# Attention of a four-stage chain: value products issued for one unit at a time in place of two, with other preferences in the plan of instruction order

## The chip, the cores and the metric

The kernel runs on one core of a Trainium2 chip. The metric is device time of one execution in microseconds (us); the kernel before took 3964.82 us (median of three runs, 3960.57 to 3975.85). The profiled execution took 3958.41 us, and the span of its trace, from the first instruction to the last, is 3956.8 us.

## The reference, cut to what matters

Four layers run one after the other on 4096 tokens of 256 channels, each with a residual and a layer norm: a recurrent scan, a mixture of experts, causal attention, a second mixture of experts. The change touches attention alone:

```python
q_lat = (x @ Wq_down).reshape(b, t, H, L)      # H = 16 heads; k_lat, v_lat likewise
...
q = jnp.concatenate([q_c, _apply_rope(q_e, cos, sin)], axis=-1)   # 16 channels a head
k = jnp.concatenate([k_c, _apply_rope(k_e, cos, sin)], axis=-1)
scores = jnp.einsum('bhqd,bhkd->bhqk', q, k) * scale
scores = jnp.where(causal[None, None], scores, -jnp.inf)
att = jax.nn.softmax(scores, axis=-1)
y = jnp.einsum('bhqk,bhkd->bhqd', att, v)
```

Here b is 1 and t is 4096.

## The kernel before

Attention works on two heads at a time: eight pairs of heads, and in each pair the 4096 queries in eight chunks of 512. A *segment* is two chunks of one pair (in the middle of the stage an early one with a late one, so that each segment has the same work); there are 32. A *unit* is one chunk of 512 queries against 128 keys, for both heads; there are 1152, and a middle segment has 36. The four units of a chunk that lie on the causal diagonal use fewer columns and add a mask with two small matmuls for each head.

Each score is computed twice on TensorE. First *S* (L1598, masks at L1604): 128 queries against 512 keys, for both heads, into two PSUM banks, of which VectorE takes the row maximum (L1724). S has a ring of two such pairs of banks (RING_S), so S number i waits for the maximum of number i-2. At the end of a segment its maxima are negated, turned by a transpose (L1652), copied by ScalarE (L1683) and sent through memory into two extra rows of the queries. Then *ST* (L1622, masks at L1627): the transposed scores of one head of a unit, less the maximum, into one bank; ScalarE takes the exponential into probs_T (L1677). ST has a ring of three banks (RING_ST), shared with the transposes of the maxima, so an ST waits for the exponential three items earlier. Last *AV* (`values`, L1642): the value products, probs_T as the moving operand against 17 columns of values (16 channels and a one, which gives the sum of the row). The two heads and the two halves of the 512 queries lie in four column groups of the array, so four matmuls run side by side; each is two instructions in the trace, so a full unit has eight. In the lists of instruction order each is one, so a full unit has four there. AV waits for the exponentials of its units; an exponential waits until AV has read the buffer it writes (a ring of six units, RING_P). ScalarE copies a finished chunk out (L1689).

S and ST use 64-row parts of the array, one head in each, so two heads run side by side. AV uses all rows and 32-column parts.

In which order TensorE, ScalarE and VectorE issue all this is laid down beforehand by `attention_plan()`. It plays the stage through with estimated durations. At each step it lists what TensorE could issue next, each with its earliest start and a due time: for ST the time at which ScalarE runs out of work, for S the time at which VectorE does, for AV a fixed time from now (REACT) less a sum for each unit by which AV lags. Of those that could start within SOON of the earliest it takes the one that is due first. On the chip the order is fixed, and semaphores set the times. S may run up to two segments ahead of ST.

Of the kernel before, what the change touches and what calls it, by code (L numbers as in the profile page):

```python
# [1265 lines left out]
NSEG = NPH * len(MIDDLE)  # L1266
SEGMENTS = RISING + (NPH - 2) * MIDDLE + RISING[::-1]
RING_P = 6
WIDE_S = 2
RING_S = 2  # L1270
S_BANKS = WIDE_S * RING_S
RING_ST = 7 - S_BANKS
# [31 lines left out]
def attention_plan():  # L1304

    units, rows = attention_units()
    SEEN, SOON = 80, 200
    LATENCY, LANDED, CLOSE, REACT = 270, 6000, 900, 2500
    last_row = {n: r for r, (n, x, i, m) in enumerate(rows)}
    n_s = len(rows) * 2 // WIDE_S
    n_t = len(units) * 2
    pe, half, act, dve = 0, [0, 0], 0, 0
    st = av = s = turn = 0
    item, consumed, exped, maxed = 0, {}, {}, {}  # L1320
    av_end, o_copied, folded, landed = {}, 0, {}, {}
    order_pe, order_dve, order_act = [], [], []
    to_act, to_dve = [], []

    def stream(start, j, columns, diag):
        begin = max(start, half[j])
        half[j] = begin + 30 + 0.42 * columns + (110 if diag else 0)
        return half[j] + LATENCY

    while True:  # L1330

        while to_act or to_dve:
            queues = [(max(q[0][0], t), name) for q, t, name in ((to_act, act, "act"), (to_dve, dve, "dve")) if q]
            start, name = min(queues)
            if start >= pe:
                break
            ready, kind, x, cost = (to_act if name == "act" else to_dve).pop(0)
            end = start + cost
            if name == "act":
                act = end  # L1340
                order_act.append((kind, x))
                if kind == "EXP":
                    consumed[x[1]] = end
                    exped[x[0]] = end
                elif kind == "MCOPY":
                    consumed[x[1]] = end
                    landed[x[0]] = end + LANDED
                else:
                    o_copied = end
            else:  # L1350
                dve = end
                order_dve.append((kind, x))
                maxed[x] = end
                r, heads = heads_of_S(x)
                n = rows[r][0]
                if r == last_row[n] and heads[-1] == 1:
                    dve += CLOSE
                    order_dve.append(("MFIN", n))
                    folded[n] = dve
        can = []  # L1360
        if st < n_t and 2 * av > st // 2 - RING_P and (item < RING_ST or item - RING_ST in consumed):
            n = units[st // 2][0]
            if n in landed:
                ready = max(landed[n], consumed[item - RING_ST] + SEEN if item >= RING_ST else 0)
                can.append((max(pe, ready), act + sum(w[3] for w in to_act), "ST", st))
        if 4 * av + 3 < st and (4 * av + 3) in exped:
            n, qc, kt = units[2 * av]
            if kt or not any(w[1] == "OCOPY" for w in to_act):
                ready = max(exped[4 * av + 3], o_copied if kt == 0 else 0) + SEEN
                can.append((max(pe, ready, max(half)), pe + REACT - 100 * (st // 2 - 2 * av - 2), "AV", av))  # L1370
        if s < n_s and (s < RING_S or s - RING_S in maxed) and (st == n_t or rows[heads_of_S(s)[0]][0] <= units[st // 2][0] + 2):
            ready = maxed[s - RING_S] + SEEN if s >= RING_S else 0
            can.append((max(pe, ready), dve + sum(w[3] for w in to_dve), "S", s))
        if turn in folded and (item < RING_ST or (item - RING_ST) in consumed):
            ready = max(folded[turn], consumed[item - RING_ST] if item >= RING_ST else 0) + SEEN
            can.append((max(pe, ready), pe - 2000, "MTURN", turn))
        if not can:
            if not to_act and not to_dve:
                if landed and st < n_t and units[st // 2][0] not in landed:
                    raise ValueError("stuck")  # L1380
                return order_pe, order_act, order_dve, max(pe, act, dve)
            pe = max(pe, min(max(q[0][0], t) for q, t in ((to_act, act), (to_dve, dve)) if q)) + 1
            continue
        soonest = min(c[0] for c in can)
        pending = [max(q[0][0], t) for q, t in ((to_act, act), (to_dve, dve)) if q]
        if pending and min(pending) < soonest:
            pe = max(pe, min(pending) + 1)
            continue
        start, _, kind, x = min((c for c in can if c[0] <= soonest + SOON), key=lambda c: c[1])
        if kind == "ST":  # L1390
            n, qc, kt = units[x // 2]
            columns = CH - max(0, kt - QT * qc) * P
            ready = stream(start, head_of_T(x), columns, kt >= QT * qc)
            pe = max(start, half[head_of_T(x)] - 240) + 60
            to_act.append((ready, "EXP", (x, item), 30 + columns / 0.954))
            item += 1
            st += 1
        elif kind == "AV":
            pe = start + 60
            for n, qc, kt in units[2 * x:2 * x + 2]:  # L1400
                pe += 2 * 0.91 * min(HALF, CH - max(0, kt - QT * qc) * P)
            half[:] = [pe, pe]
            av_end[x] = pe + 100
            av += 1
            if kt == QT * qc + QT - 1:
                to_act.append((pe + 300, "OCOPY", (n, SEGMENTS[n].index(qc)), 350))
        elif kind == "S":
            r, heads = heads_of_S(x)
            n, _, i, m = rows[r]
            columns = min(CH, (i + 1) * P - m * CH)  # L1410
            for j in heads:
                ready = stream(start, j, columns, m == i // QT)
                start = max(start, half[j] - 240) + 60
            pe = start
            to_dve.append((ready, "MAX", x, (60 + len(heads) * columns) / 0.96))
            s += 1
        else:
            pe = max(start, max(half)) + 120
            half[:] = [pe, pe]
            to_act.append((pe + LATENCY, "MCOPY", (x, item), 250))  # L1420
            item += 1
            turn += 1
        order_pe.append((kind, x))


def attention(nc, k, a):
# [5 lines left out]
    units, rows = attention_units()  # L1432
# [3 lines left out]
    slots, item = {}, 0  # L1436
# [10 lines left out]
    last_row = {n: r for r, (n, x, i, m) in enumerate(rows)}  # L1447
    s_before = {n: (last_row[n] + 1) * 2 // WIDE_S for n in range(NSEG)}
    chunk_of = {(n, x): 2 * n + x for n in range(NSEG) for x in range(2)}
    last_group = {(n, SEGMENTS[n].index(qc)): u // 2 for u, (n, qc, kt) in enumerate(units)}  # L1450
    with ExitStack() as ctx:
        sb, sem = k.sbuf(ctx), k.stage_sem
        q = sb("q_rows", [P, 2, T], F32R)
# [15 lines left out]
        st_done, taken, av_done, o_copied = (sem("at_" + n) for n in ("st_done", "taken", "av_done", "o_copied"))  # L1469
# [109 lines left out]
        def _(pe):  # L1579
# [48 lines left out]
                last.then_inc(st_done, 1)  # L1628

            def values(g):  # L1630
                pe.wait_ge(taken, slots["ST", 4 * g + 3] + 1)
                for u in (2 * g, 2 * g + 1):
                    n, qc, kt = units[u]
                    c = chunk_of[n, SEGMENTS[n].index(qc)]
                    if kt == 0 and c:
                        pe.wait_ge(o_copied, c)
                    for j in range(2):
                        for half in range(2):
                            lo = max(0, max(0, kt - QT * qc) * P - HALF * half)
                            if lo < HALF:  # L1640
                                at = 32 * (2 * j + half)
                                last = pe.matmul(ps[at:at + HD + 1, 7, lo:HALF], k.v[:, kt, 2 * (n // 4) + j, :],  # L1642
                                                 pt[:, u % RING_P, j, HALF * half + lo:HALF * (half + 1)],
                                                 start=(kt == 0), stop=(kt == QT * qc + 1 + 2 * half))
                last.then_inc(av_done, 1)
# [19 lines left out]
        def _(act):  # L1665
            for c in range(4):
                load_first(act, kk, 1, (HIGH, HIGH, LOW), c)
            for kind, x in plan_act:
                if kind == "EXP":
                    t, at_item = x  # L1670
                    u, j = t // 2, head_of_T(t)
                    n, qc, kt = units[u]
                    o = max(0, kt - QT * qc) * P
                    act.wait_ge(st_done, at_item + 1)
                    if u >= RING_P:
                        act.wait_ge(av_done, (u - RING_P) // 2 + 1)
                    act.activation(pt[:, u % RING_P, j, o:CH], ps[:, S_BANKS + at_item % RING_ST, o:CH], ACT.Exp, scale=SCALE).then_inc(taken, 1)  # L1677
                elif kind == "MCOPY":
                    n, at_item = x
# [542 lines left out]
```

## Time and profile before

| | before |
|---|---|
| median of three runs | 3964.82 us |
| profiled execution, span of its trace | 3958.41 us, 3956.8 us |
| attention, from the first S to the last AV | 1630.3 to 3208.6 us |
| busy over the span: TensorE, VectorE, ScalarE | 83%, 75%, 50% |
| S matmuls, ST matmuls, AV matmuls (records) | 2304, 2304, 8704 |
| maxima on VectorE, exponentials on ScalarE | 1152, 2304 |

A matmul's record reaches from its start to a modelled end, and matmuls overlap in the array; so how long TensorE is held by one is read from the distance of one start to the next.

### The profile page before, as it was taken

Reading aid. Unit: us, or ns where it says so; the run is one execution under the profiler, and the core shown is the slowest. Engines: PE = TensorE matmul, PEld = TensorE weight load, DVE = VectorE, ACT = ScalarE, POOL = GpSimd, SP = SyncE. Lnnn points to the kernel's source line nnn. Section 1 sums busy time; section 2 is a strip of 40 time slices with the busy share of each in tenths; the row PEclk is TensorE's granted clock in tenths of the full one; section 3 lists DMA queues with packets and bytes.
Section 4 is the critical chain, followed back from the end, with each engine's and each line's share of the span. In section 5 each row is a group of like instructions: output and inputs, shape, how many; then the busy total and the mean of one; then the engine's idle time right before and its main releaser. Section 6 shows DMA issues by size and latency. Waiting matters only on the chain. (4 is left out here: it accounts for less than half of the span.)

```text
span 3956.8 us, 70342 instructions
## 1 busy us (share of the span) xinstructions
PE 3296.1 (83%) x25130; PEld 2356.1 (60%) x25130; DVE 2956.1 (75%) x5189; ACT 1989.2 (50%) x4068; POOL 1121.4 (28%) x1381
## 2 busy tenths in 40 slices
PE   4477776780799956799999999999999955999997
PEld 1477776740688855544555555555555424888886
DVE  7999999941344446688888888888889406888888
ACT  2544444410444412256777777777777832333333
POOL 2888888705222242000111111112021030000000
PEclk7788888875899967788999999999999977999999
DMA  3000000012222135520303031221200000000001
GB/s 135 1 1 0 0 0 0 0 46 105 94 85 85 53 100 158 119 38 7 45 13 45 13 45 24 36 35 26 42 18 11 9 24 9 13 12 12 12 12 43
DMA packets 85212, 150.95 MB, mean 38 GB/s; under 512 B 16625, under 2 KB 53382, under 8 KB 83251
## 3 DMA queue, kind: packets, MB, share of 16 engines
q1 hardware_dynamic: 64626, 104.12, 10.9%
q0 software_dynamic: 19584, 42.14, 3.5%
q10 hardware_dynamic: 768, 1.57, 0.3%
q8 instruction: 146, 2.39, 0.3%
q14 instruction: 88, 0.71, 0.1%
HBM read 90.60 MB, written 57.41 MB: 37 GB/s over the span
## 5 line engine op out<-in xcount | busy, mean ns | idle before, releaser
L1724 DVE TENSOR_REDUCE row_max<-psum 128x2 f32<-128x1024 f32 (+2 forms) x1152 | 1250.4, 1131 | 219.1 <-PE psum L1598 164.2
L1677 ACT ACTIVATE probs_T<-psum 128x512 f32<-128x512 f32 (+3 forms) x2304 | 1120.8, 566 | 366.0 <-PE psum L1622 283.6
L1622 PE MATMUL psum<-q_rows,k_rows 50*128 50x512 f32 (+3 forms) x2304 | 771.6, 440 | 15.1 <-ACT probs_T L1677 11.5
L379 PE MATMUL psum<-h_hist,stream 128*128 128x192 f32 x2816 | 502.8, 344 | 246.4 <-ACT h_hist L360 246.4
L1598 PE MATMUL psum<-k_rows,q_rows 48*128 48x512 f32 (+3 forms) x2304 | 641.1, 451 | 39.3 <-DVE row_max L1724 23.8
L334 POOL TENSOR_TENSOR x_times_b<-x_slab,B_sb 128x384 f32<-128x384 f32 (+1 forms) x828 | 625.4, 818 | 149.3 <-DVE psum L285 91.1
L379 PEld LDWEIGHTS psum<-h_hist,stream 128*128 128x128 f32 x2816 | 496.4, 203 | 252.7 <-ACT h_hist L360 154.6
L1642 PE MATMUL psum<-probs_T,v_all 128*17 128x256 f32 (+1 forms) x8704 | 600.3, 378 | 1.0 <-issue 1.0
L1622 PEld LDWEIGHTS psum<-q_rows,k_rows 50*128 50x128 f32 x2304 | 364.7, 187 | 328.5 <-ACT probs_T L1677 278.3
L360 ACT ACTIVATE h_hist<-psum 128x384 f32<-128x384 f32 (+1 forms) x828 | 339.4, 453 | 378.4 <-DVE psum L285 378.4
L1972 PE MATMUL psum<-x_T,w_part 128*128 128x512 f32 x1632 | 404.3, 397 | 24.8 <-POOL w_part L2032 24.8
L1598 PEld LDWEIGHTS psum<-k_rows,q_rows 48*128 48x128 f32 x2304 | 286.9, 191 | 151.7 <-DVE row_max L1724 96.3
L285 DVE TENSOR_TENSOR psum<-psum,x_times_b 128x384 f32<-128x384 f32 (+1 forms) x828 | 372.9, 508 | 0.0
L280 DVE TENSOR_TENSOR psum<-h_hist,psum 128x384 f32<-128x384 f32 (+1 forms) x828 | 371.2, 506 | 0.5 <-ACT h_hist L360 0.2
L1642 PEld LDWEIGHTS psum<-probs_T,v_all 128*17 128x17 f32 x8704 | 210.5, 97 | 259.4 <-ACT probs_T L1677 80.9
L1972 PEld LDWEIGHTS psum<-x_T,w_part 128*128 128x128 f32 x1632 | 301.0, 190 | 85.5 <-POOL w_part L2032 24.9
L1567 POOL DMA_DIRECT2D o_raw<-o_acc x64 | 37.0, 578 | 1092.1 <-ACT o_acc L1689 1057.6
L2071 DVE SCALAR_TENSOR_TENSOR stream<-psum,comb,stream 128x256 f32<-128x256 f32 x544 | 236.4, 476 | 0.6 <-PE psum L1984 0.6
L1984 PEld LDWEIGHTS psum<-w_part,hidden_T 128*128 128x128 f32 x1632 | 214.4, 192 | 28.6 <-DVE hidden_T L2057 15.6
L1984 PE MATMUL psum<-w_part,hidden_T 128*128 128x256 f32 x1632 | 219.4, 285 | 14.2 <-DVE hidden_T L2057 14.2
L832 PE MATMUL psum<-xeT_part,w_part 128*128 128x512 f32 x768 | 183.2, 398 | 25.4 <-ACT hT_part L873 12.8
L2032 POOL TENSOR_TENSOR w_part<-attn_T,w_part 128x768 fp32r<-128x768 f32 x17 | 31.5, 1853 | 599.1 <-ACT w_part L1996 493.7
(212 smaller groups left out, 3260.2 us busy)
## 6 DMA issues: line engine op xcount, KB each, us to landing
w_raw<-in_w SPq DMA_DIRECT2D x16, 1024.0 KB, 8.4
qk_rows<-qk_split SPq DMA_DIRECT2D x64, 256.0 KB, 3.0
q_rows<-qk_rows SPq DMA_DIRECT2D x42, 256.0 KB, 12.0
k_rows<-qk_rows SPq DMA_DIRECT2D x42, 256.0 KB, 16.8
inbox<-zeros SPq DMA_DIRECT2D x8, 1024.0 KB, 10.5
xe_sb<-inbox SPq DMA_DIRECT2D x8, 1024.0 KB, 6.0
outbox<-ye_sb POOLq DMA_DIRECT2D x8, 1024.0 KB, 10.4
o_raw<-o_acc POOLq DMA_DIRECT2D x64, 128.0 KB, 2.1
```

The source lines that it names most:

```text
L280: dve.tensor_tensor(part(ha, i), part(prev, i), over_chunks(A, i), ALU.mult).then_inc(ha_ready, 1)
L285: dve.tensor_tensor(u(i), part(ha, i), part(xb[:, t % RING_X], i), ALU.add).then_inc(u_ready, 1)
L334: pool.tensor_tensor(out, x, b, ALU.mult).then_inc(xb_ready, 1)
L360: act.activation(part(hist[:, slot, t], i), u(i), ACT.Tanh).then_inc(h_ready, 1)
L379: last = pe.matmul(ps[:, 1 + j, 0:BL * DH * CHUNKS], diag[:, s, :], hist[:, j, :, :, :].rearrange("p t h (s c) -> p (t h) s c", s=NS)[:, : ...
L1598: last = pe.matmul(ps[:, bank_of_S(s, j), 0:width], q[at, b, i * P:(i + 1) * P], kk[at, b, mm * CH:mm * CH + width], start=True, stop=not ...
L1622: last = pe.matmul(ps[:, bank, o:CH], kk[at, b, kt * P:(kt + 1) * P], q[at, b, qc * CH + o:(qc + 1) * CH], start=True, stop=not diag)
L1642: last = pe.matmul(ps[at:at + HD + 1, 7, lo:HALF], k.v[:, kt, 2 * (n // 4) + j, :], pt[:, u % RING_P, j, HALF * half + lo:HALF * (half + 1 ...
L1677: act.activation(pt[:, u % RING_P, j, o:CH], ps[:, S_BANKS + at_item % RING_ST, o:CH], ACT.Exp, scale=SCALE).then_inc(taken, 1)
L1724: dve.tensor_reduce(mx[:, n % 4, heads[0]:heads[-1] + 1, QT * c + i % QT, mm], ps[:, banks, 0:width], AX.X, ALU.max).then_inc(maxed, 1)
L1972: last = pe.matmul(ps[:, 2 * half + c % 2, :], w_part[:, b, wp, at:at + INTER], xT[:, xp, h, c * CH:(c + 1) * CH], start=(n == 0 and h == ...
L1984: last = pe.matmul(ps[:, 4 + 2 * (c % 2) + s // 2, (s % 2) * D:(s % 2 + 1) * D], hT[:, c % 2, hp, s * P:(s + 1) * P], w_part[:, b, wp, WCO ...
```

## The change

AV is issued for one unit in place of two (GROUP = 1), and the waits on either side follow: AV waits for two exponentials in place of four, and an exponential waits for the AV of one unit. In the plan the window in which items compete, SOON, goes from 200 to 100, the due time of AV, REACT, from 2500 to 1000, and each unit of lag brings AV forward by 300 in place of 100. The number of matmuls, maxima and exponentials is the same; lines from 1266 on move by one or two.

```diff
+GROUP = 1
...
-    SEEN, SOON = 80, 200
-    LATENCY, LANDED, CLOSE, REACT = 270, 6000, 900, 2500
+    SEEN, SOON = 80, 100
+    LATENCY, LANDED, CLOSE, REACT = 270, 6000, 900, 1000
...
-        if st < n_t and 2 * av > st // 2 - RING_P and (item < RING_ST or item - RING_ST in consumed):
+        if st < n_t and GROUP * av > st // 2 - RING_P and (item < RING_ST or item - RING_ST in consumed):
...
-        if 4 * av + 3 < st and (4 * av + 3) in exped:
-            n, qc, kt = units[2 * av]
+        last_exp = 2 * GROUP * (av + 1) - 1
+        if last_exp < st and last_exp in exped:
+            n, qc, kt = units[GROUP * av]
...
-                can.append((max(pe, ready, max(half)), pe + REACT - 100 * (st // 2 - 2 * av - 2), "AV", av))
+                can.append((max(pe, ready, max(half)), pe + REACT - 300 * (st // 2 - GROUP * av - 2), "AV", av))
...
             def values(g):
-                pe.wait_ge(taken, slots["ST", 4 * g + 3] + 1)
-                for u in (2 * g, 2 * g + 1):
+                pe.wait_ge(taken, slots["ST", 2 * GROUP * (g + 1) - 1] + 1)
+                for u in range(GROUP * g, GROUP * (g + 1)):
...
-                        act.wait_ge(av_done, (u - RING_P) // 2 + 1)
+                        act.wait_ge(av_done, (u - RING_P) // GROUP + 1)
```

On TensorE in a stretch of full units in the middle of the stage (L1622 is ST, one head in a row without a count; L1598 is S, both heads; L1642 is AV), before:

```order
L1622 MATMUL psum<-q_rows,k_rows 128x512
L1598 MATMUL psum<-k_rows,q_rows 128x512 x2
L1622 MATMUL psum<-q_rows,k_rows 128x512 x2
L1598 MATMUL psum<-k_rows,q_rows 128x512 x2
L1622 MATMUL psum<-q_rows,k_rows 128x512
L1642 MATMUL psum<-probs_T,v_all 17x256 x8
```

and such a stretch in the changed kernel, where ST is L1624, S is L1600 and AV is L1644:

```order
L1624 MATMUL psum<-q_rows,k_rows 128x512
L1600 MATMUL psum<-k_rows,q_rows 128x512 x2
L1624 MATMUL psum<-q_rows,k_rows 128x512
L1644 MATMUL psum<-probs_T,v_all 17x256 x4
L1624 MATMUL psum<-q_rows,k_rows 128x512 x2
L1644 MATMUL psum<-probs_T,v_all 17x256 x4
L1600 MATMUL psum<-k_rows,q_rows 128x512 x2
L1624 MATMUL psum<-q_rows,k_rows 128x512 x2
L1644 MATMUL psum<-probs_T,v_all 17x256 x4
```

Where four ST and two S stood between two runs of AV, now two ST and one S or none stand there.

On TensorE near the end of the stage, when no S is left, before:

```order
L1642 MATMUL psum<-probs_T,v_all 17x256 x2
L1642 MATMUL psum<-probs_T,v_all 17x128 x2
L1622 MATMUL psum<-q_rows,k_rows 128x512 x3
L1642 MATMUL psum<-probs_T,v_all 17x256 x8
L1622 MATMUL psum<-q_rows,k_rows 128x512 x3
L1642 MATMUL psum<-probs_T,v_all 17x256 x8
L1622 MATMUL psum<-q_rows,k_rows 128x512 x4
```

and in the changed kernel:

```order
L1624 MATMUL psum<-q_rows,k_rows 128x512 x3
L1644 MATMUL psum<-probs_T,v_all 17x256 x8
L1624 MATMUL psum<-q_rows,k_rows 128x512 x2
L1644 MATMUL psum<-probs_T,v_all 17x256 x4
L1624 MATMUL psum<-q_rows,k_rows 128x512 x2
L1644 MATMUL psum<-probs_T,v_all 17x256 x4
L1624 MATMUL psum<-q_rows,k_rows 128x512 x2
```

Runs of four ST and eight AV become runs of two ST and four AV; where two AV units follow each other without anything between (x8), the order keeps a run of two. Counted over the whole order of TensorE, AV stands in 575 unbroken runs before and in 987 after, 165 of which hold two units. The maxima on VectorE keep their order; on ScalarE the exponentials keep theirs, and the copies of finished chunks and of turned maxima move among them.

## Rows read from the trace of the kernel before

**Rows 1.** Windows: attention in four stretches, busy time of each engine, TensorE's clock.

```profile
core 0: us, PE busy (x) PEld busy (x) DVE busy (x) ACT busy (x) POOL busy (x), PEclk, DMA share, GB/s
1630.28:1901.18 270.90, 246.46 (x2104) 126.90 (x2104) 234.21 (x237) 145.03 (x301) 11.83 (x18) 0.83 0.18 26
1901.18:3028.17 1126.99, 1119.18 (x11540) 591.06 (x11537) 964.55 (x989) 861.17 (x1800) 184.47 (x264) 1.00 0.18 31
3028.17:3106.74 78.57, 78.31 (x814) 40.27 (x811) 64.32 (x68) 60.61 (x124) 7.73 (x11) 1.00 0.03 9
3106.74:3208.60 101.86, 93.60 (x949) 44.40 (x945) 12.20 (x19) 82.33 (x177) 20.14 (x31) 1.00 0.06 16
```

**Rows 2.** Waits, second stretch: who waited for whom, us, times, longest.

```profile
PEld psum L1622 <- ACT probs_T L1677: 200.6, 520, 1.6
ACT probs_T L1677 <- PE psum L1622: 196.8, 345, 1.9
...
DVE row_max L1724 <- PE psum L1598: 134.5, 256, 4.0
```

**Rows 3.** Timeline, no S left: start, us, engine, line, idle before and its releaser.

```profile
3141.11 0.73 PE L1622 MATMUL psum<-q_rows,k_rows 50*128 50x512 f32 x3
3141.64 2.06 ACT L1677 ACTIVATE probs_T<-psum 128x512 f32<-128x512 f32 x4 [0.52 <-PE psum L1622]
...
3142.29 0.50 PE L1622 MATMUL psum<-q_rows,k_rows 50*128 50x512 f32 x1 [0.45 <-ACT probs_T L1677]
...
3142.72 1.06 PE L1642 MATMUL psum<-probs_T,v_all 128*17 128x256 f32 x16
...
3143.71 0.73 PE L1622 MATMUL psum<-q_rows,k_rows 50*128 50x512 f32 x3
```

**Rows 4.** Timeline of PE in the second stretch, one period and a shorter AV run.

```profile
2344.08 1.06 PE L1642 MATMUL psum<-probs_T,v_all 128*17 128x256 f32 x16
2345.07 0.49 PE L1622 MATMUL psum<-q_rows,k_rows 50*128 50x512 f32 x1
2345.07 0.72 PE L1598 MATMUL psum<-k_rows,q_rows 48*128 48x512 f32 x2
2345.41 0.62 PE L1622 MATMUL psum<-q_rows,k_rows 50*128 50x512 f32 x2
2345.77 0.50 PE L1598 MATMUL psum<-k_rows,q_rows 48*128 48x512 f32 x2
2346.25 0.50 PE L1622 MATMUL psum<-q_rows,k_rows 50*128 50x512 f32 x1
2346.68 1.06 PE L1642 MATMUL psum<-probs_T,v_all 128*17 128x256 f32 x16
...
2351.36 0.84 PE L1642 MATMUL psum<-probs_T,v_all 128*17 128x256 f32 x12
```

**Rows 5.** Timeline of PE, second stretch, a period with no idle step.

```profile
2301.06 1.06 PE L1642 MATMUL psum<-probs_T,v_all 128*17 128x256 f32 x16
2302.05 0.50 PE L1598 MATMUL psum<-k_rows,q_rows 48*128 48x512 f32 x2
2302.38 0.40 PE L1622 MATMUL psum<-q_rows,k_rows 50*128 50x512 f32 x2
2302.61 0.40 PE L1598 MATMUL psum<-k_rows,q_rows 48*128 48x512 f32 x2
2302.85 0.39 PE L1622 MATMUL psum<-q_rows,k_rows 50*128 50x512 f32 x1
2303.17 1.06 PE L1642 MATMUL psum<-probs_T,v_all 128*17 128x256 f32 x16
```

**Rows 6.** Groups by form, second stretch: count, busy us, mean ns, idle before.

```profile
L1724 DVE TENSOR_REDUCE row_max<-psum 128x2 f32<-128x1024 f32 x728 | 860.4, 1220 | 140.8 <-PE psum L1598 134.5 <-PE psum L1604 4.0
L1677 ACT ACTIVATE probs_T<-psum 128x512 f32<-128x512 f32 x1440 | 747.8, 602 | 215.3 <-PE psum L1622 196.8 <-PE psum L1627 17.1
```

More of the change, by code:

```diff
@@ L1365, in attention_plan @@
                 can.append((max(pe, ready), act + sum(w[3] for w in to_act), "ST", st))
-        if 4 * av + 3 < st and (4 * av + 3) in exped:
-            n, qc, kt = units[2 * av]
+        last_exp = 2 * GROUP * (av + 1) - 1
+        if last_exp < st and last_exp in exped:
+            n, qc, kt = units[GROUP * av]
             if kt or not any(w[1] == "OCOPY" for w in to_act):
-                ready = max(exped[4 * av + 3], o_copied if kt == 0 else 0) + SEEN
-                can.append((max(pe, ready, max(half)), pe + REACT - 100 * (st // 2 - 2 * av - 2), "AV", av))
+                ready = max(exped[last_exp], o_copied if kt == 0 else 0) + SEEN
+                can.append((max(pe, ready, max(half)), pe + REACT - 300 * (st // 2 - GROUP * av - 2), "AV", av))
         if s < n_s and (s < RING_S or s - RING_S in maxed) and (st == n_t or rows[heads_of_S(s)[0]][0] <= units[st // 2][0] + 2):
@@ L1399, in attention_plan @@
             pe = start + 60
-            for n, qc, kt in units[2 * x:2 * x + 2]:
+            for n, qc, kt in units[GROUP * x:GROUP * (x + 1)]:
                 pe += 2 * 0.91 * min(HALF, CH - max(0, kt - QT * qc) * P)
@@ L1449, in attention @@
     chunk_of = {(n, x): 2 * n + x for n in range(NSEG) for x in range(2)}
-    last_group = {(n, SEGMENTS[n].index(qc)): u // 2 for u, (n, qc, kt) in enumerate(units)}
+    last_group = {(n, SEGMENTS[n].index(qc)): u // GROUP for u, (n, qc, kt) in enumerate(units)}
     with ExitStack() as ctx:
```

## The prediction

> **What bounds the kernel now.** I read the windows first, to see how much of the span the change can touch. Attention runs from 1630.28 to 3208.60 us, four stretches of together 1578 us [rows 1]; the other 2380 us of the profiled execution hold no instruction that moves. The second stretch, 1127 us, is 24 like segments of 36 units, so 864 units at 1.304 us, or 2.61 us for each AV run of two. TensorE looks full there, 1119 of 1127 us, VectorE stands at 965 and ScalarE at 861 [rows 1]. A reader who stops here calls TensorE the bound.
>
> The waits deny it: in that stretch ST's weight loads waited 201 us for exponentials, exponentials 197 us for ST, maxima 135 us for S [rows 2]. Engines that wait for each other go round in a ring, and the timeline shows which. Clearest is the end of the stage, where VectorE has nothing to do [rows 3]: three ST start at 3141.11 when AV is through, the first exponential starts 0.53 us later, the fourth ST starts 0.65 us after that (0.60 us of exponential [rows 6] and 0.05 us of signal), AV 0.43 us after the fourth ST, and the next ST 0.99 us after AV. The sum is 2.60 us, and the fourth ST has its engine idle for 0.45 us, released by ScalarE. The ring is of three banks, a run of AV needs four ST, so the fourth cannot go before the exponential of the first, and AV comes behind it. In the middle of the stage the same stands with S in between [rows 4]: AV at 2344.08, ST 2345.07, last ST 2346.25, AV 2346.68, again 2.60 us, which is the mean of the whole stretch. Where only three ST lie between two AV runs, TensorE never stands and a period takes 2.11 us [rows 5], with four slots like the other. So it is the ring that bounds, and TensorE gives 0.49 us in each 2.60 us to it, 432 x 0.49 = 212 us in the second stretch.
>
> The Trainium skill, page "Perfetto Trace Analysis", section "Engine Utilization", warns against the same reading: matmul busy time misleads because matmuls are pipelined. Here 99% busy goes with 19% of standing, so the trace agrees.
>
> **The change, part by part.** *What goes.* With two ST between AV runs, the ring no longer closes in a run: an ST needs the exponential three items earlier, 0.53 + 0.60 + 0.05 = 1.18 us after that ST's start [rows 3, 6], and in three items, one and a half units, TensorE now has at least 1.8 us of its own work (below). So I let the 212 us go, and ask what is late next.
>
> *What comes.* Each break between AV and the rest costs TensorE time, and this the trace shows. Slots of S or ST in a row are 0.23 to 0.24 us apart; the last slot before AV takes 0.32, the first after AV 0.33 us [rows 5]. A run of sixteen AV records takes 0.99 us to the next ST, of which each four take 0.22 us (1.06 less 0.84 for twelve [rows 4]), 0.88 in all and 0.11 for the end. Together 0.09 + 0.10 + 0.11 = 0.30 us for each run. Runs go from 575 to 987 in the stage and from 432 to 727 in the second stretch: 295 x 0.30 = 88 us there. Semaphore waits of AV (one for each unit) have nothing to price: in the new order, at least five ST, over two units, stand between the ST of the last exponential needed and AV for 990 of 1152 units.
>
> *TensorE's new need in the second stretch.* Before: 432 x 2.11 = 912 us. After: 912 + 88 = 1000 us. The other way: a unit with its own run needs 0.55 (AV of eight records, 0.99 - 0.44) + 0.33 + 0.32 = 1.20 us, 864 x 1.205 = 1041 us, less 137 runs saved by doubles, 41 us: 1000 again. VectorE is next: 965 us busy, 860.4/728 = 1.18 us for each full maximum [rows 1, 6]; ScalarE's 861 us is covered. Two engines at 1.16 and 1.12 us a unit, joined by a ring of two S, don't run without loss, and diagonal units and turned maxima leave slots of one head empty. A period with all slots used and every run single, 1041 us, is the row-based figure nearest to what order shows most (822 of 987 runs are single); with 2% for such losses I take 1062 us, 65 us less than 1127. Ends: 1000 us (no wait left) and 1127 + 88 = 1215 us (no wait freed).
>
> *Third stretch*, 60 units, 78.6 us, 1.31 us each: the same ratio, 4 us less. *Fourth stretch*, 101.9 us, mostly the ring alone. Now the second ST of a unit waits for the first exponential of the unit before: one turn, two units, is 1.18 + 0.43 + 0.55 = 2.16 us, 1.08 for a unit against 1.30. With some 45 of 84 units full and in that pattern: 45 x 0.22 = 10 us less; I take 9. *First stretch*, 270.9 us for 144 units: its waits are for maxima that come through memory and for S alone (VectorE 234 us), with the clock at 0.83 on average, so partly at 1.2 GHz. It has 57 more runs, 17 us at full clock and up to twice that at half, and its full units gain 0.10 us each as in the middle. I take 2 us less, between -12 and +15. *Exponentials waiting for AV's buffers* (ring of six units) are released a unit sooner, not later. *Copies on ScalarE*, 64 and 32 in the stage, only move among the exponentials, which leave that engine 266 us free in the second stretch [rows 1]. SP and POOL issue what they did, each released by the same copies.
>
> Sum: -65 - 4 - 9 - 2 = -80 us. The profiled execution goes from 3958.4 to 3878 us; the median of the runs shown lies 6 us above it, so I forecast 3885 us.
>
> **The rivals.** *Slower: TensorE is the bound already.* If the 212 us of standing come back in other places (S waiting on VectorE, which then runs at a busy share of 0.9), the added breaks lie on the path: at worst 412 x 0.30 = 124 us, 4082 us. It decides from the point where less than 88 of the 212 us are freed. For it: TensorE's 99% and the 135 us that VectorE already waits for S [rows 1, 2]. Against it: rows 3, where VectorE is out of play and the period is the same 2.60 us. By the Trainium skill, page "TensorEngine Tiling (Array Packing)", section "Tiling Modes", a change of tiling mode, not merely of tile, drains the array; this is the page's case against the change, since S and ST use row parts and AV column parts. Rows 4 and 5 agree, with about 0.30 us for a run's two changes. Chance 0.10.
>
> *No change.* The old ring goes, but the two engines left almost without slack, 1000 and 965 us, lose 0.10 us a unit to each other through the two S buffers: 864 x 1.30 again, so 3958 us and some 9 us less for the end: 3950 to 3965. For it: 256 of the stretch's 869 maxima wait today [rows 2]. Against it: AV, which keeps S away for 0.99 us now, keeps it away for 0.55 us, less than the 1.18 us of one maximum. Chance 0.12.
>
> *All of the waiting goes.* Second stretch at 1000 us, third at 70, fourth at 87: 127 + 9 + 15 = 151 us less, 3807 us and some 3814 on the scale of the median. For it, the even rows of the new order; against it, diagonal units. Chance 0.08.
>
> **How the numbers follow.** The forecast itself has 0.70, with 3840 to 3940 us as its range (losses of 0 to 5% on 1041 us, and the first stretch either way). Range over the cases: 3835 to 3960, which leaves out the slower rival and most of the full gain. A measurement of this kernel tells about 0.5%, 20 us, from no change: faster is below 3945 (0.70 + 0.08), slower above 3985 (0.10), and 0.12 between.
>
> **What would show it.** If right: in the second stretch a segment of 36 units takes about 44 us in place of 46.9; the ST that is released by ScalarE after an idle step is gone from the rows of full units; periods of one unit are about 1.2 us with AV to ST at 0.55 us; waits of maxima for S fall from 135 us or stay in spite of shorter time; the end of the stage, after the last S, shrinks by about 10 us. Wrong in size: AV to ST above 0.55 us, so that a run of one costs more than the rows of runs of two tell. Wrong in kind: PE idle released by VectorE at S where it was ScalarE at ST, with periods still at 1.3 us a unit.

## The result and the profile after

The changed kernel took 3941.94 us (median of six runs, 3927.57 to 3944.87) against 3967.21 us (six runs) before: a ratio of 0.9933, 95% interval 0.9912 to 0.9953, so 25 us or 0.7% faster. The profiled execution took 3940.81 us, 17.6 us less than the one of before. I had forecast 3885 us, a gain of 80.

The windows of the four stretches, cut at the same places of the program (first S, first ST of segments 4, 28 and 29, last AV), answer to [rows 1]; columns as there:

```profile
1629.36:1925.08 295.72, 270.70 (x2110) 119.03 (x2110) 237.63 (x236) 150.13 (x301) 11.84 (x18) 0.74 0.16 24
1925.08:3017.62 1092.54, 1090.85 (x11533) 504.97 (x11529) 977.91 (x987) 881.76 (x1800) 184.40 (x264) 1.00 0.19 32
3017.62:3093.63 76.01, 76.01 (x796) 34.27 (x792) 67.84 (x67) 62.36 (x122) 7.70 (x11) 1.00 0.03 9
3093.63:3190.40 96.77, 96.77 (x970) 40.73 (x966) 13.03 (x24) 83.26 (x178) 20.14 (x31) 1.00 0.06 17
```

| stretch | before, us | after, us | change forecast | change measured |
|---|---|---|---|---|
| first (S alone, then small segments) | 270.9 | 295.7 | -2 | **+24.8** |
| second (24 like segments) | 1127.0 | 1092.5 | -65 | **-34.5** |
| third | 78.6 | 76.0 | -4 | -2.6 |
| fourth | 101.9 | 96.8 | -9 | -5.1 |

So 42 us were gained and 25 of them given back in a stretch that I had called neutral. The timeline of TensorE in the second stretch, as in [rows 4, 5], has the period that I forecast:

```profile
2415.83 0.63 PE L1644 MATMUL psum<-probs_T,v_all 128*17 128x256 f32 x8
2416.39 0.50 PE L1600 MATMUL psum<-k_rows,q_rows 48*128 48x512 f32 x2
2416.73 0.40 PE L1624 MATMUL psum<-q_rows,k_rows 50*128 50x512 f32 x2
2417.06 0.63 PE L1644 MATMUL psum<-probs_T,v_all 128*17 128x256 f32 x8
2417.62 0.50 PE L1600 MATMUL psum<-k_rows,q_rows 48*128 48x512 f32 x2
2417.96 0.39 PE L1624 MATMUL psum<-q_rows,k_rows 50*128 50x512 f32 x2
2418.27 0.62 PE L1644 MATMUL psum<-probs_T,v_all 128*17 128x256 f32 x8
```

From the start of AV to the start of S it is 0.56 us. A slot (one S or ST for both heads) takes 0.34 us when it is the first after AV and 0.33 when it is the last before the next AV, so a unit takes 1.22 us (2417.06 to 2418.27: 1.21); forecast were 0.55, 0.33, 0.32 and 1.20. No step stands waiting for ScalarE: with the exponentials halved (below) these periods stay at 1.22 us. The waits of the stretch answer to [rows 2]:

```profile
PEld psum L1624 <- ACT probs_T L1679: 134.1, 339, 0.4
...
ACT probs_T L1679 <- PE psum L1624: 99.4, 235, 1.4
DVE row_max L1726 <- PE psum L1600: 80.4, 173, 1.6
```

The longest wait of ST for an exponential was 1.6 us and is 0.4 us, no more than the weight load of an S stands idle behind AV when it waits for nothing (0.42 us at 2416.39); VectorE's longest wait went from 4.0 to 1.6 us. At the end of the stage two units take 2.23 us (forecast 2.16, before 2.60):

```profile
3125.47 0.50 PE L1624 MATMUL psum<-q_rows,k_rows 50*128 50x512 f32 x2
...
3125.90 0.63 PE L1644 MATMUL psum<-probs_T,v_all 128*17 128x256 f32 x8
3126.00 2.07 ACT L1679 ACTIVATE probs_T<-psum 128x512 f32<-128x512 f32 x4 [0.16 <-PE psum L1624]
...
3126.45 0.70 PE L1624 MATMUL psum<-q_rows,k_rows 50*128 50x512 f32 x2
...
3127.14 0.63 PE L1644 MATMUL psum<-probs_T,v_all 128*17 128x256 f32 x8
...
3127.70 0.50 PE L1624 MATMUL psum<-q_rows,k_rows 50*128 50x512 f32 x2
```

Most of what the first stretch lost lies in its second segment (28 units; 55.0 us before, 70.1 after), and another 8 us in its first. Windows of the second segment from its first ST on, before:

```profile
1689.31:1700.00 10.69, 10.69 (x63) 5.57 (x59) 8.06 (x8) 6.84 (x13) 0.00 (x0) 0.50 0.96 110
1700.00:1722.00 22.00, 22.00 (x227) 11.80 (x223) 19.26 (x18) 16.94 (x36) 0.57 (x1) 1.00 0.54 67
```

and after:

```profile
1697.10:1719.00 21.90, 21.90 (x133) 9.58 (x129) 12.89 (x12) 11.12 (x21) 0.00 (x0) 0.50 0.99 116
1719.00:1741.00 22.00, 22.00 (x126) 9.44 (x124) 11.18 (x10) 10.38 (x22) 0.57 (x1) 0.51 0.02 7
```

Before, TensorE ran 11 us of this work at 1.2 GHz and then at 2.4; after, 44 us at 1.2 GHz, with its records as full as ever, 22.00 of 22 us, and little more than half the instructions. Over the whole first stretch the mean clocks, 0.83 of 270.9 us and 0.74 of 295.7 us, make about 92 us at 1.2 GHz before and 154 after (an estimate, with the clock at one of two levels). I had not thought that the change could move the clock.

### The profile page after: what moved, and what is told of

Read it like the earlier page. It is cut to its first block and busy times, and to the rows that moved or that the text cites. A ratio compares the mean times of both kernels' runs of the same rounds, so it can differ in the third digit from the quotient of the medians.

```text
span 3939.2 us, 70342 instructions
## 1 busy us (share of the span) xinstructions
PE 3311.8 (84%) x25130; PEld 2271.2 (58%) x25130; DVE 2976.9 (76%) x5189; ACT 2018.1 (51%) x4068; POOL 1121.9 (28%) x1381
## 3 DMA queue, kind: packets, MB, share of 16 engines
q8 instruction: 146, 2.39, 0.3%
## 5 line engine op out<-in xcount | busy, mean ns | idle before, releaser
L1726 DVE TENSOR_REDUCE row_max<-psum 128x2 f32<-128x1024 f32 (+2 forms) x1152 | 1271.7, 1134 | 187.5 <-PE psum L1600 126.9
L1679 ACT ACTIVATE probs_T<-psum 128x512 f32<-128x512 f32 (+3 forms) x2304 | 1155.5, 562 | 326.1 <-PE psum L1624 176.3
L379 PE MATMUL psum<-h_hist,stream 128*128 128x192 f32 x2816 | 520.1, 352 | 228.9 <-ACT h_hist L360 228.9
L1644 PE MATMUL psum<-probs_T,v_all 128*17 128x256 f32 (+1 forms) x8704 | 692.8, 386 | 1.3 <-issue 1.3
L1600 PE MATMUL psum<-k_rows,q_rows 48*128 48x512 f32 (+3 forms) x2304 | 648.9, 469 | 36.7 <-DVE row_max L1726 21.8
L1624 PE MATMUL psum<-q_rows,k_rows 50*128 50x512 f32 (+3 forms) x2304 | 676.0, 433 | 3.3 <-DMA q_rows<-max_parts 3.3
L379 PEld LDWEIGHTS psum<-h_hist,stream 128*128 128x128 f32 x2816 | 513.7, 209 | 235.2 <-ACT h_hist L360 138.4
L1624 PEld LDWEIGHTS psum<-q_rows,k_rows 50*128 50x128 f32 x2304 | 330.5, 190 | 250.8 <-ACT probs_T L1679 204.5
L1600 PEld LDWEIGHTS psum<-k_rows,q_rows 48*128 48x128 f32 x2304 | 278.6, 194 | 257.6 <-issue 164.1
L1974 PE MATMUL psum<-x_T,w_part 128*128 128x512 f32 x1632 | 404.4, 397 | 24.8 <-POOL w_part L2034 24.8
L285 DVE TENSOR_TENSOR psum<-psum,x_times_b 128x384 f32<-128x384 f32 (+1 forms) x828 | 384.4, 551 | 0.0
L280 DVE TENSOR_TENSOR psum<-h_hist,psum 128x384 f32<-128x384 f32 (+1 forms) x828 | 382.8, 548 | 0.5 <-ACT h_hist L360 0.2
L1644 PEld LDWEIGHTS psum<-probs_T,v_all 128*17 128x17 f32 x8704 | 169.2, 96 | 306.6 <-ACT probs_T L1679 163.5
L1986 PEld LDWEIGHTS psum<-w_part,hidden_T 128*128 128x128 f32 x1632 | 215.5, 193 | 27.5 <-DVE hidden_T L2059 14.5
```

Source lines behind the costliest of these rows:

```text
L280: dve.tensor_tensor(part(ha, i), part(prev, i), over_chunks(A, i), ALU.mult).then_inc(ha_ready, 1)
L285: dve.tensor_tensor(u(i), part(ha, i), part(xb[:, t % RING_X], i), ALU.add).then_inc(u_ready, 1)
L379: last = pe.matmul(ps[:, 1 + j, 0:BL * DH * CHUNKS], diag[:, s, :], hist[:, j, :, :, :].rearrange("p t h (s c) -> p (t h) s c", s=NS)[:, : ...
L1600: last = pe.matmul(ps[:, bank_of_S(s, j), 0:width], q[at, b, i * P:(i + 1) * P], kk[at, b, mm * CH:mm * CH + width], start=True, stop=not ...
L1624: last = pe.matmul(ps[:, bank, o:CH], kk[at, b, kt * P:(kt + 1) * P], q[at, b, qc * CH + o:(qc + 1) * CH], start=True, stop=not diag)
L1726: dve.tensor_reduce(mx[:, n % 4, heads[0]:heads[-1] + 1, QT * c + i % QT, mm], ps[:, banks, 0:width], AX.X, ALU.max).then_inc(maxed, 1)
```

## The experiments

Stretches of every profiled execution, cut in the same way (us; clock is the granted clock of the first stretch, 1.0 being 2.4 GHz; ratio to the kernel before, where timed in rounds; the kernels with half exponentials or no masks leave work out and ran once):

| kernel | clock | first | second | third | fourth | ratio, 95% |
|---|---|---|---|---|---|---|
| before | 0.83 | 270.9 | 1127.0 | 78.6 | 101.9 | |
| changed | 0.74 | 295.7 | 1092.5 | 76.0 | 96.8 | 0.9933 (0.9912-0.9953) |
| pairs, new preferences | 0.82 | 280.1 | 1155.0 | 81.6 | 145.4 | 1.0158 (1.0115-1.0202) |
| singles, old preferences | 0.69 | 304.3 | 1161.8 | 77.8 | 98.1 | 1.0082 (1.0052-1.0111) |
| singles, REACT alone new | 0.66 | 327.2 | 1153.3 | 79.8 | 97.1 | 1.0115 (1.0082-1.0148) |
| changed, S doubled | 0.77 | 287.3 | 1103.9 | 76.1 | 96.8 | 0.9920 (0.9893-0.9946) |
| before, S doubled | 0.82 | 274.5 | 1126.5 | 78.6 | 101.8 | 1.0001 (0.9983-1.0019) |
| before, half exponentials | 0.82 | 262.9 | 1099.3 | 76.6 | 94.4 | |
| changed, half exponentials | 0.74 | 290.9 | 1093.5 | 75.9 | 90.3 | |
| before, no masks | 0.81 | 268.1 | 1099.5 | 77.2 | 105.6 | |
| changed, no masks | 0.72 | 286.3 | 1049.6 | 72.8 | 93.2 | |
| hybrid | 0.80 | 277.8 | 1089.7 | 76.0 | 96.8 | 0.9868 (0.9842-0.9894) |
| hybrid, costs in the plan | 0.81 | 275.0 | 1112.8 | 76.8 | 94.4 | 0.9918 (0.9899-0.9937) |

**Group and preferences apart.** Pairs with the new preferences:

```diff
-GROUP = 1
+GROUP = 2
```

> Runs of AV stay at two units (576 runs against 575 before); only the preferences (SOON 100, REACT 1000, weight 300) are those of the change. Theory (the ring of three ST banks bounds runs of two; the group size makes the change): four ST still stand between most runs, so periods of full units stay at 2.60 us and the second stretch at 1127 us within 15; whole kernel within 0.5% of before. Rival (the preferences, not the group, brought the second stretch's 35 us): second stretch near 1092 us.

Singles with the old ones:

```diff
-    SEEN, SOON = 80, 100
-    LATENCY, LANDED, CLOSE, REACT = 270, 6000, 900, 1000
+    SEEN, SOON = 80, 200
+    LATENCY, LANDED, CLOSE, REACT = 270, 6000, 900, 2500
...
-                can.append((max(pe, ready, max(half)), pe + REACT - 300 * (st // 2 - GROUP * av - 2), "AV", av))
+                can.append((max(pe, ready, max(half)), pe + REACT - 100 * (st // 2 - GROUP * av - 2), "AV", av))
```

> AV one unit at a time with the preferences of before; AV stands in 1141 runs against 987 in the changed kernel and 575 before. Theory: the ring is open as in the changed kernel; full units take about 1.22 us wherever a unit has its own run, and fewer units share a run; second stretch 1090 to 1130 us, kernel 0 to 30 us slower than the changed one. Rival (the number of breaks alone sets the time, 0.30 us for each of the 154 runs more): 46 us slower than the changed kernel, near 3985 us.

With REACT 1000, but SOON 200 and the weight 100:

> One unit at a time with only REACT at the new 1000; SOON 200 and weight 100 as before. AV stands in 1140 runs, like with all the old preferences. Theory (what the new preferences bring is fewer breaks, 987 runs, and S spread evenly): without the doubles about 0.30 us for each of 154 runs is lost against the changed kernel, and S comes more evenly than with REACT 2500 (1 unit in 4 of AV gaps has no S there); second stretch 1110 to 1150 us, kernel 3960 to 3990 us. Rival (REACT alone makes the gain): second stretch near 1092 us, kernel near 3940 us.

Each part alone makes the kernel slower, by 0.8 to 1.6%; of the parts tried, only group and preferences together gain. All three expectations missed. Pairs were to stay where they were and lost 28 us in the second stretch. Singles with the old preferences were to lose little and took 4000.49 us, nearer to the rival, which counts breaks alone (near 3985), than to the theory. With REACT alone the second stretch came just above its range (1153 us against 1110 to 1150), but the kernel took 4014.66 us and not 3960 to 3990.

With single units and the old preferences a full unit with one S takes 1.22 us here too. Breaks make much of the loss: in the second stretch this kernel has 864 runs of AV, the one with REACT alone 861 and the changed kernel 727, and at 0.30 us a run that is about 40 us of the 69 and 61 us by which the two are longer (an estimate). The rest I put down to S. With the old preferences VectorE's timeline shows holes of 7.0 to 8.2 us between two maxima, 22 of them in the second stretch, about one in each segment:

```profile
2211.68 0.25 DVE L1703 RECIPROCAL o_inverse<-o_sums 128x16 f32<-128x16 f32 x1
2219.18 1.02 DVE L1726 TENSOR_REDUCE row_max<-psum 128x2 f32<-128x256 f32 x2 [7.26 <-PE psum L1606]
```

S has run ahead to its limit of two segments (the S before this hole is the last of segment 11), and TensorE works off ST and AV with no S among them up to the last ST of segment 9. But the holes are worth little: with REACT alone they are gone, and the second stretch is only 8.5 us shorter. VectorE's waits for S with all the old preferences, and then with REACT alone:

```profile
DVE row_max L1726 <- PE psum L1600: 149.8, 105, 7.3
```

```profile
DVE row_max L1726 <- PE psum L1600: 116.2, 257, 1.8
```

With pairs and the new preferences the four ST stay between the runs, and the fourth stretch shows 145 us where TensorE's clock is 0.66 on average (1.00 before), so half of what this kernel loses in the profiled execution lies there and not in the second stretch:

```profile
3146.81:3292.16 145.35, 135.66 (x949) 55.36 (x945) 13.45 (x19) 83.16 (x176) 23.10 (x33) 0.66 0.04 12
```

So no single preference tried, nor the size alone, made the gain: it is the order that both make.

**The ring of three ST banks.** Exponentials over half of their columns, in both kernels (probs_T is set to one beforehand, so that the other half holds numbers):

```diff
-                    act.activation(pt[:, u % RING_P, j, o:CH], ps[:, S_BANKS + at_item % RING_ST, o:CH], ACT.Exp, scale=SCALE).then_inc(taken, 1)
+                    act.activation(pt[:, u % RING_P, j, o:(o + CH) // 2], ps[:, S_BANKS + at_item % RING_ST, o:(o + CH) // 2], ACT.Exp, scale=SCALE).then_inc(taken, 1)
```

> The kernel before with exponentials over the first half of their columns only (the other half of probs_T stays at 1, so the output is not the reference's); order and matmuls as before. Theory (the ring of three ST banks, closed by the first exponential, sets the 2.60 us): the exponential goes from 0.60 to about 0.39 us and the period by as much, to 2.39 us, where the two maxima (2.36) are next; second stretch near 1040 us, periods of the end from 2.60 to 2.39 us. Rival (S and the maxima set the period): 2.60 us and 1127 us stay.

> The changed kernel with the same half exponentials. Theory (TensorE's own slots set its 1.22 us for each unit): full units stay at 1.22 us, second stretch 1070 to 1095 us, less than a third of what the kernel before gains. Rival (ScalarE still closes a ring in the changed kernel): the second stretch gains 60 us or more.

The kernel before, the same place of the order as [rows 4]:

```profile
2333.40 1.06 PE L1643 MATMUL psum<-probs_T,v_all 128*17 128x256 f32 x16
...
2335.36 0.50 PE L1623 MATMUL psum<-q_rows,k_rows 50*128 50x512 f32 x1
2335.79 0.41 PE L1643 MATMUL psum<-probs_T,v_all 128*17 128x256 f32 x4
```

2.39 us in place of 2.60, as forecast: the first exponential did set this period. But the stretch shrank by 28 us, not by 87. The traces tell why, if TensorE's timeline of the second stretch is cut at each start of a run of AV and the periods are sorted:

| periods, kernel before | how many | total, us | total with half exponentials, us |
|---|---|---|---|
| four ST, two S, no mask, as [rows 4] | 138 | 359.7 | 339.9 |
| with mask matmuls | 229 | 637.5 | 628.6 |
| all others | 64 | 127.0 | 128.1 |

Only 138 of the 431 whole periods are of the kind that I had read; their median is 2.60 us and with half exponentials 2.39, and they give back 20 of the 28 us. More than half of the stretch is periods with mask matmuls, and those hardly follow the exponential. So the ring set the full periods, not the stretch.

The changed kernel's second stretch did not move at all, 1093.5 against 1092.5 us: ScalarE no longer bounds it. In the fourth stretch, where the ring still turns once in two units, the same edit took 6.5 us (96.8 to 90.3).

**TensorE as the new bound.** Both lines of mask matmuls left out:

```diff
-                diag = mm == i // QT
+                diag = False
...
-                diag = kt >= QT * qc
+                diag = False
```

> The changed kernel without the causal mask's matmuls (both lines are left out, so the diagonal blocks are not masked). In the second stretch that takes 1536 small matmuls from TensorE, in pairs on two halves, each pair about 0.11 us for one half of two: some 42 us of its time. Theory (TensorE bounds the second stretch): 1045 to 1065 us in place of 1092. Rival (VectorE, whose work stays, bounds it): above 1080 us.

> The kernel before without the causal mask's matmuls (both lines are left out, so the diagonal blocks are not masked). Theory (the ring and the maxima bound it, TensorE stands for a fifth): second stretch 1100 to 1125 us in place of 1127, so well under the 43 us that the changed kernel gained. Rival (TensorE bounded before too): 1085 us or less.

The second stretch of the changed kernel without masks, and then of the kernel before without them:

```profile
1912.72:2962.32 1049.60, 1045.74 (x10016) 451.97 (x10013) 971.83 (x987) 880.23 (x1800) 184.48 (x264) 1.00 0.20 33
```

```profile
1899.79:2999.25 1099.46, 1083.83 (x10020) 526.42 (x10016) 962.04 (x989) 856.76 (x1800) 184.50 (x264) 0.99 0.19 31
```

The changed kernel's went to 1049.6 us, 43 less, as a stretch bound by TensorE should, with VectorE's work nearly unchanged (972 us busy, 978 with masks). The kernel before got 27.5 us shorter, half a microsecond past the edge of what I expected, though the clock cost it something (0.99 in place of 1.00). So it was bound in part by TensorE before too, in the periods with masks, but less than the changed kernel.

**The clock in the first stretch.** First an attempt to keep TensorE busy where S runs alone (`again` holds the S that stand in unbroken runs of six or more, all in the first stretch; 40 small matmuls also run before the first S):

```diff
+                if s in again:
+                    for j in heads:
+                        at = slice(64 * j, 64 * j + SROWS)
+                        pe.matmul(ps[:, bank_of_S(s, j), 0:width], q[at, b, i * P:(i + 1) * P], kk[at, b, mm * CH:mm * CH + width],
+                                  start=True, stop=True)
```

> The changed kernel, with TensorE given more to do where only S is issued in the first stretch: in unbroken runs of at least six S each pair of S matmuls is issued twice into the same bank, and 40 small matmuls run before the first S. Theory (the first stretch lost 25 us because TensorE stands at 1.2 GHz there for longer, and needs more of it): its clock in the stretch up to 1925 us rises from 0.74 to above 0.85, and the stretch shrinks from 296 us to 265 to 275; kernel 20 to 30 us faster than the changed one. Rival (the stretch is longer because of its 57 added runs and the new order, whatever the clock): clock up, stretch within 8 us of 296.

> The kernel before with the same addition. Theory: clock in the first stretch from 0.83 to above 0.9, stretch 255 to 268 us in place of 271; the difference of the two warmed kernels in the first stretch is under 8 us, where it is 25 us without. Rival: the two differ by some 25 us as before.

It did not do what it was for: the mean clock came to 0.77 and 0.82, not above 0.85 and 0.9, and the two kernels differ by 13 us in the first stretch, between theory (under 8) and rival (25). But in the second segment, where the changed kernel had lost most, it tells something. There the same order of single units is back at 2.4 GHz after 12 us in place of 44:

```profile
1706.87:1718.87 12.00, 12.00 (x71) 4.75 (x67) 7.21 (x8) 6.66 (x13) 0.00 (x0) 0.50 1.04 120
1718.87:1741.00 22.13, 22.13 (x224) 10.40 (x216) 19.08 (x18) 16.91 (x36) 0.57 (x1) 1.00 0.44 55
```

and the segment takes 58.4 us, where the changed kernel took 70.1 and the kernel before 55.0. So of the 15 us lost in this segment about 12 go with the clock. (Its second stretch is 11 us longer than the changed kernel's; there the clock fell once, to 0.50 from 2493.8 to 2514.2 us.)

Then pairs in the old order for the first 144 units (PAIRED) and singles with the new preferences after them:

```diff
+    groups = [(u, u + 2) for u in range(0, PAIRED, 2)] + [(u, u + 1) for u in range(PAIRED, n)]
...
+        SOON, REACT, LAG = (200, 2500, 100) if done < PAIRED else (100, 1000, 300)
```

> The first 144 units (segments 0 to 3) in pairs with the preferences of before, all later ones one at a time with the new ones; TensorE's order is that of before up to the end of the first stretch. Theory (in the first stretch the change lost 25 us because TensorE, at 1.2 GHz after each stretch of S alone, comes back to 2.4 GHz later with single runs; the rest of the stage gained 43): first stretch 268 to 276 us at a clock near 0.83, second 1085 to 1105, the rest as in the changed kernel; kernel 15 to 30 us faster than the changed one, near 3917 us. Rival (the first stretch's loss is start-up that differs from run to run): first stretch near 296 us again, no faster than the changed kernel.

It took 3915.5 us (3906.93 to 3926.11), near the 3917 expected. All six runs lie below every run of the changed kernel, and of the kernels here that leave nothing out it is the fastest. The first stretch is 277.8 us, a little above the range, at a clock of 0.80. Its windows have the clock back by 1719 us; its second segment began at 1699.9:

```profile
1719.00:1741.00 22.00, 22.00 (x234) 11.35 (x235) 20.03 (x19) 15.02 (x32) 0.57 (x1) 1.00 0.13 20
```

The loss is not start-up that varies: six profiles in which the first stretch has single units show 286 to 327 us at 0.66 to 0.77, seven with pairs 263 to 280 us at 0.80 to 0.83. In the second segment the clock is back after 6 to 13 us in all seven with pairs, and after 25 to 47 us in five of the six with singles; the sixth is the one with S doubled. That the order decides how long TensorE stays at 1.2 GHz is shown; by what, is not. How much of the whole stretch's 18 us is the clock and how much the 57 added breaks by themselves is shown for the second segment alone.

**Fewer breaks.** The hybrid with the costs of a break in the plan, 784 runs of AV:

```diff
+        before = order_pe[-1][0] if order_pe else kind
+        if before == "AV" and kind != "AV" and done >= PAIRED:
+            half[:] = [max(pe, max(half)) + 200] * 2
+        elif before != "AV" and kind == "AV" and done >= PAIRED:
+            start += 90
```

> The hybrid (pairs in the first 144 units), with two costs added to the plan from unit 144 on: 0.09 us before and 0.20 us after each run of AV, as the trace shows them. The plan then makes 784 runs of AV against 928 in the hybrid; between two runs mostly three ST, so single and double runs take turns. Theory (TensorE bounds the second stretch, and each break costs 0.30 us; three ST don't close the ring): up to 130 runs fewer there, 39 us less of TensorE's time, of which VectorE at 1.18 us for each full maximum lets half through: second stretch 1065 to 1080 us in place of 1090, kernel near 3897 us. Rival (TensorE's waits, not its breaks, are what is left): no gain or a loss, 3910 to 3935 us.

The rival was right: 3931.6 us, and a second stretch of 1112.8 us against the hybrid's 1089.7, although 144 breaks are gone. Part of these 23 us goes with the clock. Early in the stretch TensorE stood for 2.35 us inside a run of AV, for nothing that the profile shows, and then ran at 1.2 GHz for 17 us:

```profile
1919.78 1.04 PE L1660 MATMUL psum<-probs_T,v_all 128*17 128x256 f32 x4 [2.35 <-issue]
```

```profile
1920.00:1937.00 17.00, 17.00 (x100) 7.27 (x97) 8.73 (x8) 7.63 (x15) 7.09 (x10) 0.50 0.35 56
```

The first two segments of the stretch are 12 us longer than in the hybrid. Segments 6 to 23 have the full clock in both; the hybrid, and then the hybrid with costs:

```profile
2003.73:2821.81 818.08, 818.08 (x8665) 381.41 (x8662) 732.11 (x745) 661.03 (x1350) 138.45 (x198) 1.00 0.17 30
```

```profile
2001.52:2826.03 824.51, 820.68 (x8657) 401.63 (x8655) 716.65 (x738) 651.87 (x1351) 138.30 (x198) 1.00 0.17 29
```

There, too, fewer breaks gained nothing, and cost 6 us. VectorE waited for S, over the whole stretch, in the hybrid and then here:

```profile
DVE row_max L1737 <- PE psum L1611: 79.6, 178, 1.6
```

```profile
DVE row_max L1742 <- PE psum L1616: 113.6, 176, 3.8
```

As many waits, but longer ones. That each pair of AV that saves a break keeps S away for longer would explain them; no run takes it apart.

## Why the prediction was wrong

The direction, the ring in the full periods, its opening, the price of a break and the 1.20 us period were right, these two within 0.03 us. The steps that failed are terms of the sum.

*First stretch, -2 us with bounds of -12 and +15; measured +24.8.* I took the share of the stretch at 1.2 GHz [rows 1] as given. It grew: the order with single units returned to 2.4 GHz after 44 us of the second segment where the old one needed 11. The bound let the added breaks cost double, but held the time at low clock fixed. The hybrid takes back 18 us of it.

*Second stretch, -65 us; measured -34.5.* The step that failed is "A period with all slots used and every run single, 1041 us, ... with 2% for such losses". It priced diagonal units like full ones and left out their 1536 mask matmuls. The run without them comes within 1% of that figure, 1049.6 us; the masks are 43 us when TensorE bounds. That it comes so near is luck in part, since 137 of the 727 runs in this stretch hold two units and not one. The figure of 1000 us, which credits 41 us to these runs, was further off. The last experiment shows that a break saved need not be time saved; the two kernels with 864 and 861 runs suggest that over 130 more of them do cost it.

*The freed standing, 212 us.* The same mistake stands on the side of before. I multiplied the 0.49 us of one period by all 432, because its 2.60 us is also "the mean of the whole stretch". It is a mean of unlike periods: 138 of 2.61 us, 229 with masks of 2.78 and 64 of 1.98. For most of them neither the standing nor the 2.11 us of TensorE's need had been read. So the 19% of standing that the prediction sets beside 99% busy is that of the full period, not of the stretch. The warning about busy time that it takes there from the Trainium skill, page "Perfetto Trace Analysis", stands in the section "Identifying the Most-Contended Engine", not in "Engine Utilization". The gain of 34.5 us and 88 us for added breaks make about 122 us that came free in place of 212 (an estimate, if each break costs 0.30 us).

GROUP = 1 with the old preferences opened the ring as well and lost 35 us in the second stretch: it has a run of AV for every unit. I had read the preferences as a detail of the plan and did not ask what the order would be without them; they were as decisive as the group. Third and fourth stretch erred by 1.4 and 3.9 us.

Of the rivals, "TensorE is the bound already" asked for less than 88 us freed in the second stretch, and the stretch gained, though the kernel before without masks shows that TensorE bounded part of it. "No change" (3950 to 3965 us) came nearer in size than the forecast, but not by its mechanism: the second stretch did gain, and the first gave it back.

## What to carry to other kernels

A ring closes where one engine's batch needs more buffers than the ring has: count the items between two batches against the ring before pricing engines. Then count how many periods are of the kind that was read (here 138 of 431) before multiplying its wait by all of them; a mean that agrees with one period proves nothing. When the ring opens, the next bound must be summed with everything on that engine, the small masking matmuls too. And look at the clock of the stretch in which the engine is coming back from idleness: an order that is better at 2.4 GHz can keep TensorE at 1.2.

## What the runs showed of the hardware

- TensorE at 1.2 GHz with its records at 100% busy for 44 us did not return to 2.4 GHz while AV came in single runs; in the old order it returned after 11 us of the same work. With each S issued twice where S ran alone, it returned after 12 us with single runs too, though the mean clock of the first stretch rose only from 0.74 to 0.77.
- In the fourth stretch of pairs with the new preferences the clock fell to 0.66 on average, with TensorE 93% busy by its records (135.66 of 145.35 us), and the stretch took 145 us in place of 102. Why it fell is not shown.
- In the hybrid with costs TensorE stood for 2.35 us inside a run of AV, and the clock was then 0.50 for 17 us. What stopped it is not shown.
- A break between row parts and column parts of the array costs 0.30 us in all: 0.11 at the end of AV, 0.10 at the first slot, 0.09 at the last, the same for runs of one unit and of two.
